# Four warming matmuls instead of nine, filter rows early, and V kept per row: a reordered prologue of a deformable-convolution and spectral-filter kernel

## The reference, cut to what matters

```python
x = x + _L0_conv_ref(_ln_c(x), offset_w, offset_b, mask_w, mask_b, weight, gamma, beta, mean, var)
t = _to_tokens(x)
t = t + _L0_ffn_ref(_ln_t(t), sigma, phi, M_u, M_phi_plus, M_phi_minus, log_weights, gumbel)
x = _from_tokens(t, x)
...
# in _L0_conv_ref: sample 4 corners for each of 9 taps at learned offsets, weigh by ly, lx and a mask
out = deform_conv2d(x, offset, mask, weight, s, p)
scale = bn_gamma / jnp.sqrt(bn_var + BN_EPS)
out = (out - bn_mean) * scale + bn_beta
return out * jax.nn.sigmoid(out)
# in _L0_ffn_ref, for four branches of different length, chosen by a softmax with a hard maximum
s = sigma ** 0.25
out = einsum('btkd,k,kde->bte', U_plus, s, Mpp) + einsum('btkd,k,kde->bte', U_minus, s, Mpm)
out = out + sum_i einsum('btd,de->bte', shift(u, i), Mu[i])          # i = 0, 1, 2
```

## Time and profile before

| what | us |
|---|---|
| median of 3 runs (754.41 to 762.09) | 757.35 |
| profiled execution, its own time | 751.24 |
| span of the profiled execution | 749.4 |
| mean granted TensorE clock | 0.784 |
| busy in the span: PE, PEld, DVE, ACT, POOL | 506.5, 376.8, 314.9, 179.7, 292.7 |
| the chain that ended last: PE, unknown queue, issue, DVE, ACT | 55%, 25%, 10%, 5%, 4% |

### The profile page before, as it was taken

How to read it: one execution, slowest core, us unless ns; L and a number is a source line. 1 busy time by engine, 2 the same in 40 slices (tenths; PEclk the granted TensorE clock), 3 DMA queues, 4 the chain that set the end, 5 groups by cost and what they waited for, 6 DMA issues and landing times.

```text
span 749.4 us, 13126 instructions
## 1 busy us (share of the span) xinstructions
PE 506.5 (68%) x5598; PEld 376.8 (50%) x5598; DVE 314.9 (42%) x800; ACT 179.7 (24%) x421; POOL 292.7 (39%) x295
## 2 busy tenths in 40 slices
PE   5976429246208845785889549891168648999998
PEld 3443105135106613564678329771156327788997
DVE  6467411868602703850438007187009025753000
ACT  1121012113004302321232102240033113334322
POOL 1257750634770372556253732237702745000000
PEclk9966558659557966986999759996569759899999
DMA  8526373811330131222121320113300321000000
GB/s 166 127 79 158 101 204 117 282 56 50 98 105 2 46 107 45 66 71 85 44 64 37 100 64 23 44 44 98 98 21 30 105 64 56 16 2 3 9 2 9
DMA packets 43778, 54.27 MB, mean 72 GB/s; under 512 B 24664, under 2 KB 34142, under 8 KB 43721
## 3 DMA queue, kind: packets, MB, share of 16 engines
q0 software_dynamic: 13824, 37.77, 17.1%
q1 hardware_dynamic: 23841, 13.42, 6.9%
q10 hardware_dynamic: 6056, 2.26, 1.3%
HBM read 50.12 MB, written 3.30 MB: 71 GB/s over the span
## 4 chain that ended last, share of the span: by engine, by line
PE 55%; another core or an unknown queue 25%; issue 10%; DVE 5%; ACT 4%; DMA 1%; SPq 0%; ACTq 0%; DVEq 0%
PE bank L888 30%; PE bank L900 7%; PE bank L760 2%; PE bank L834 2%; PE bank L824 2%; ACT u_conv L661 2%; PE bank L793 2%; PE bank L741 1%; PE bank L795 1%; PE bank L732 1%; PE bank L845 1%; PE bank L919 1%; ACT vT L628 1%; DMA filt<-in_L_ffn_phi_dram 1%
## 5 line engine op out<-in xcount | busy, mean ns | idle before, releaser
L269 POOL DMA_INDIRECT G<-corner_table,idx x288 | 290.0, 1007 | 343.9 <-DVE idx L362 155.2
L888 PE MATMUL bank<-filt,u_hi 128*64 128x256 f16 x2560 | 255.3, 291 | 135.1 <-issue 85.6
L888 PEld LDWEIGHTS bank<-filt,u_hi 128*64 128x64 f16 x2560 | 152.8, 114 | 172.0 <-issue 112.0
L888 PE MATMUL bank<-filt,u_lo 128*64 128x256 f16 x1280 | 198.9, 291 | 15.1 <-issue 15.1
L661 ACT ACTIVATE u_conv<-bank,f_scale 128x256 f32<-128x256 f32 x256 | 118.6, 474 | 303.8 <-PE bank L888 153.6
L900 PE MATMUL bank<-u_conv,mixw 128*64 128x256 f32 (+1 forms) x640 | 94.2, 377 | 9.9 <-issue 9.2
L888 PEld LDWEIGHTS bank<-filt,u_lo 128*64 128x64 f16 x1280 | 84.3, 117 | 24.6 <-issue 22.4
L455 DVE TENSOR_TENSOR G<-G,bank 128x2304 f32<-128x2304 f32 x32 | 81.5, 2548 | 0.3
L467 DVE TENSOR_SCALAR expo<-expo 128x128 f32<-128x128 f32 x16 | 3.6, 227 | 183.1 <-ACT expo L638 172.1
L459 DVE TENSOR_TENSOR V<-G 128x576 f32<-128x576 f32 x32 | 24.3, 758 | 110.0 <-PE bank L825 73.4
L900 PEld LDWEIGHTS bank<-u_conv,mixw 128*64 128x64 f32 x640 | 47.9, 155 | 20.5 <-issue 18.9
(11 more groups left out here) (158 smaller groups left out, 387.3 us busy)
## 6 DMA issues: line engine op xcount, KB each, us to landing
filt<-filter_rows SPq DMA_DIRECT2D x16, 514.0 KB, 9.1
G<-corner_table,idx POOLq DMA_INDIRECT x288
corner_table<-n_uT SPq DMA_DIRECT2D x12, 128.0 KB, 2.9
mixw<-in_x_dram SPq DMA_DIRECT2D x2, 512.0 KB, 6.0
filt<-in_L_ffn_M_phi_plus_dram SPq DMA_DIRECT2D x8, 128.0 KB, 4.9
out_dram<-o_sb ACTq DMA_DIRECT2D x8, 128.0 KB
filt<-n_L_ffn_M_phi_minus_dram ACTq DMA_DIRECT2D x4, 128.0 KB, 4.0
corner_table<-n_uT ACTq DMA_DIRECT2D x4, 128.0 KB, 3.3
```

The costliest lines, as they stand in the source:

```text
L269: pool.indirect_dma_start(G[:, k, tap, :], None, corners[bp], bass.IndirectOffsetOnAxis(ap=idx[:, q % 2, k, tap:tap + 1], axis=0)).then_in ...
L888: last = pe.matmul(conv_ps[b2][C * src:C * src + C, 0:2 * P].rearrange("c (p a) -> c p a", p=2), u[:, NJ * bp + j2, b2, src], h, start=(j2 ...
```

## The change

The change reorders the prologue and removes some of its steps.

- `WARM_UP` is 4 instead of 9.
- The filter rows are made on DVE between the first two `positions`, and the branch weights after the second; the copy of the filter rows to HBM goes ahead of pair 1's tables in SP's queue.
- `weigh(0, 0, 0)` comes ahead of pair 1's layer norm, and `weigh(0, 0, 1)`, positions and weights of unit 1 behind it.
- `V` is kept for each row p. The write of V waits for the turn of the row before the last, and `weigh(0, 1, 0)` and `weigh(0, 1, 1)` stand ahead of the offsets of pair 1 and of both `finish`.
- The roots of the two batch-norm variances and of sigma are one chain over 128 x 80 elements (`roots`), in the place of three. `spectrum_scales` has one chain left, and stands between the two `weigh(0, 1, ...)`.
- On PE the product for the filter scales moves from ahead of row 0 to behind it.
- `u_conv` and `w_diag` share one tile (`late_tiles`), which has no instruction of its own.

```diff
-WARM_UP = 9
+WARM_UP = 4
...
-        V = sb("V", [P, 2, TAPS * C])
+        V = sb("V", [P, 2, 2, TAPS * C])
...
+        roots = sb("roots", [P, 3, C + K])
...
(sync)
+            sp.wait_ge(f_rows_ready, 1)
+            sp.dma_start(ap(hankel, 0, [[4 * HROW, K], [1, 4 * HROW]]), f_rows.rearrange("k p h c -> k (p h c)")
+                         ).then_inc(f_rows_stored, 16)
             for b2 in range(2):
                 for cy in range(2):
                     store_image(sp, 1, b2, cy)
...
-            sp.wait_ge(f_rows_ready, 1)
-            sp.dma_start(ap(hankel, 0, ...
             sp.wait_ge(f_rows_stored, 16)
             load_filters(range(8))
...
(vector)
+            def inverse_roots():
+                dve.wait_ge(s_bn, 16 * 7)
+                link(dve.tensor_scalar(roots[:, 0, 0:C], roots[:, 0, 0:C], BN_EPS, None, ALU.add))
+                rsqrt(roots[:, 1], roots[:, 0], roots[:, 2])
...
                 if b2 == 0:
-                    dve.wait_ge(val_turned, START + 2 * q + p)
-                dve.tensor_tensor(V[:, b2]...
+                    dve.wait_ge(val_turned, START + 2 * q + p - 1)
+                dve.tensor_tensor(V[:, p, b2]...
...
             branch_logits()
+            dve.memset(vT[C:C + 1, :, 4, :], 1.0).then_inc(ones_ready, 1)
             offsets(0, 0)
             positions(0, slice(0, BLK, 2))
-            branch_weights()
+            filter_rows()
             offsets(0, 1)
             positions(0, slice(1, BLK, 2))
+            branch_weights()
             masks(0)
             weights(0)
+            weigh(0, 0, 0)
+            normalise_pixels(1, (0, 1))
+            weigh(0, 0, 1)
             positions(1)
             weights(1)
-            normalise_pixels(1, (0, 1))
-            weigh(0, 0, 0)
+            inverse_roots()
             main_weights()
-            weigh(0, 0, 1)
-            filter_rows()
+            weigh(0, 1, 0)
+            spectrum_scales()
+            weigh(0, 1, 1)
             offsets(1, 0)
             offsets(1, 1)
-            dve.wait_ge(n_ready, 3)
-            dve.memset(vT[C:C + 1, :, 4, :], 1.0).then_inc(ones_ready, 1)
-            weigh(0, 1, 0)
             finish(0, 0)
-            weigh(0, 1, 1)
-            spectrum_scales()
             dve.wait_ge(f_scale_ready, 1)
...
(tensor)
-            pe.wait_ge(diag_ready, 1)
-            pe.wait_ge(off_copied, 2 * BP)
-            pe.matmul(scale_ps[:, 0:K], ones[:], f_diag[:], start=True, stop=True).then_inc(f_scale_ready, 1)
...
-            for r in range(2):
-                turn_values(r)
-                convolve_values(r)
-                turn_convolved(r)
+            turn_values(0)
+            convolve_values(0)
+            turn_convolved(0)
+            pe.wait_ge(diag_ready, 1)
+            pe.wait_ge(off_copied, 2 * BP)
+            pe.matmul(scale_ps[:, 0:K], ones[:], f_diag[:], start=True, stop=True).then_inc(f_scale_ready, 1)
+            turn_values(1)
+            convolve_values(1)
+            turn_convolved(1)
```

More of the change, by code:

```diff
@@ L108, in metaformer_kernel @@
         f_diag = sb("f_diag", [K, K])
-        sig = sb("sig", [P, 4, K])
+        sig = sb("sig", [P, 3, K])
+        roots = sb("roots", [P, 3, C + K])
         f_scale = sb("f_scale", [P, K])
         br = sb("br", [P, 10, BRANCHES])
-        w_diag = sb("w_diag", [P, BRANCHES, 3, P])
         mu_raw = sb("mu_raw", [C, BRANCHES, 3 * C])
         mu = sb("mu", [P, 4, 3, C])
-        u_conv = sb("u_conv", [P, 2, 2, 2, P])
+        late_tiles = sb("late_tiles", [P, 1536])
+        u_conv = late_tiles[:, 0:1024].rearrange("s (k b p a) -> s k b p a", k=2, b=2, p=2)
+        w_diag = late_tiles[:].rearrange("s (r v d) -> s r v d", r=BRANCHES, v=3)
         o_sb = sb("o_sb", [P, 2, 2 * P])
@@ L185, in metaformer_kernel @@
         pool_marks, pe_marks, dve_marks, act_marks = (sem(f"{n}_marks") for n in ("pool", "pe", "dve", "act"))
-        N_SMALL = 3
+        N_SMALL = 2
         N_MATS = 5 * BRANCHES
@@ L295, in _ @@
             dve.memset(ones[:], 1.0).then_inc(ones_ready, 1)
+            dve.memset(roots[:, 0, 0:C], 1.0).then_inc(roots_set, 1)
             dve.memset(f_rows, 0.0)
@@ L425, in main_weights @@
                 dve.wait_ge(s_w, 16)
-                link(dve.tensor_scalar(bn_col[:, 1:2], bn_col[:, 1:2], BN_EPS, None, ALU.add))
-                rsqrt(st2[0:C, 0, 0:1], bn_col[:, 1:2], st2[0:C, 1, 0:1])
-                link(dve.tensor_tensor(bn_col[:, 0:1], bn_col[:, 0:1], st2[0:C, 0, 0:1], ALU.mult))
+                link(dve.tensor_tensor(bn_col[:, 0:1], bn_col[:, 0:1], roots[0:C, 1, 0:1], ALU.mult))
                 dve.tensor_scalar(w_scaled[:].rearrange("o (t c) -> o t c", t=TAPS),
@@ L457, in weigh @@
                 if b2 == 0:
-                    dve.wait_ge(val_turned, START + 2 * q + p)
-                dve.tensor_tensor(V[:, b2].rearrange("s (t c) -> s t c", c=C), G[:, k, :, 0:C], G[:, k, :, C:2 * C], ALU.add
+                    dve.wait_ge(val_turned, START + 2 * q + p - 1)
+                dve.tensor_tensor(V[:, p, b2].rearrange("s (t c) -> s t c", c=C), G[:, k, :, 0:C], G[:, k, :, C:2 * C], ALU.add
                                   ).then_inc(v_ready[b2], 1)
@@ L549, in _ @@
         def _(act):
-            for i, v in enumerate((sigma, log_weights, gumbel)):
-                dst = sig[:, 0, :] if i == 0 else br[:, i - 1, :]
-                act.dma_start(dst, ap(v, 0, [[0, P], [1, K if i == 0 else BRANCHES]])).then_inc(s_small, 16)
+            for i, v in enumerate((log_weights, gumbel)):
+                act.dma_start(br[:, i, :], ap(v, 0, [[0, P], [1, BRANCHES]])).then_inc(s_small, 16)
             act.dma_start(w_raw, ap(weight, 0, [[C * TAPS, C], [1, C * TAPS]])).then_inc(s_w, 16)
-            for i, v in enumerate((gamma, var)):
-                act.dma_start(bn_col[:, i:i + 1], ap(v, 0, [[1, C], [1, 1]])).then_inc(s_bn, 16)
-            for i, v in enumerate((gamma, beta, mean, var)):
+            act.dma_start(roots[:, 0, C:C + K], ap(sigma, 0, [[0, P], [1, K]])).then_inc(s_bn, 16)
+            act.dma_start(bn_col[:, 0:1], ap(gamma, 0, [[1, C], [1, 1]])).then_inc(s_bn, 16)
+            for i, v in enumerate((gamma, beta, mean)):
                 act.dma_start(bn_row[C:C + 1, i, :], ap(v, 0, [[C, 1], [1, C]])).then_inc(s_bn, 16)
+            act.wait_ge(roots_set, 1)
+            act.dma_start(roots[0:C, 0, 0:1], ap(var, 0, [[1, C], [1, 1]])).then_inc(s_bn, 16)
+            act.dma_start(roots[C:C + 1, 0, 0:C], ap(var, 0, [[C, 1], [1, C]])).then_inc(s_bn, 16)
             for s in (u_copied, *conv_copied):
@@ L823, in turn_values @@
                     for m in range(4):
-                        pe.transpose(val_ps[b2][:, P * m:P * m + P], V[:, b2, P * m:P * m + P], ident)
-                    last = pe.transpose(tail_ps[0:C, P * b2:P * b2 + P], V[:, b2, 4 * P:4 * P + C], ident)
+                        pe.transpose(val_ps[b2][:, P * m:P * m + P], V[:, r % 2, b2, P * m:P * m + P], ident)
+                    last = pe.transpose(tail_ps[0:C, P * b2:P * b2 + P], V[:, r % 2, b2, 4 * P:4 * P + C], ident)
                 last.then_inc(val_turned, 1)
```

19 lines of the change are left out of this document (6 added, 13 removed).

## The result

The changed kernel took 767.11 us (median of 4 runs, 763.87 to 771.99); the kernel before, on the same chip beside it, 755.88 (748.04 to 762.09). The ratio is 1.018, with a 95% interval of 1.011 to 1.026: slower by 1.8%. The profiled execution of the change has a span of 766.7 us, against 749.4. The kernel before itself had medians from 756 to 770 us in the different calls, so times of different calls are compared by their ratios; where this text compares stages, it compares single traces.

What follows compares the result with a forecast made beforehand. Gather streams nearly stopping PE's hand-overs to ACT were taken as the bound. Pair 1 19 us later, rows 0 and 1 13.5 less, passes +1: +6.5, added as 6 to the median 757.35 for 763 us; range 742 to 772.

Steps and rivals of the forecast that it cites:

- Warming: Start of the prologue: ten warming pieces fewer on PE bring everything to the second indices and gather streams 3.3 us earlier.
- V per row takes POOL's pause: Prologue: DVE writes V without waiting for PE, so POOL's pause of 28.8 us between two gather streams goes.
- The stream of 63: Prologue: 45 and 18 gathers join into one stream of 81 us, from 44.8 to 126 us.
- The hold's own rule: Under gather streams: after 14 us PE's hand-overs nearly stand still, 8.8 us each; cleared about 5 us behind the last gather.
- harmless 14 us: A gather stream's first 14 us were taken not to slow PE's hand-overs to ACT, which need 2 us each there.
- Pair 1 starts at 132.5: Prologue: PE starts pair 1 behind the merged stream, 19 us later than 113.58; bounds 117 and 140.
- Rows 0 and 1: Prologue, pair 1's offsets to first convolution: row 1 is turned sooner as its V stands, 13.5 us less; bounds 10 and 15.5.
- Passes: Pass 2, unit 4: nine gathers join the 18 before them; between -2 and +4 us, taken as +1.
- Rival B: Prologue: DVE's small steps are slowed too, V comes late and breaks the long stream; no change, 757 us; chance 0.22.
- A: Prologue: the stalls don't follow the gathers, so pair 1 isn't held and the kernel is faster, 745.6 us; chance 0.27.
- C: Passes: two or three more streams merge, 11 us each; with one more such unit 774 us; chance 0.09.

Runs made afterwards that it cites:

- e4: The changed kernel with nine warming matmuls again in place of four; 782.78 us, ratio 1.026 to the kernel before.
- e11: The changed kernel run and traced once more without any edit; 778.03 us, ratio 1.011 to the kernel before.
- e1: The changed kernel, with POOL waiting after each slot's nine gathers until the last has landed; 684.97 us, ratio 0.896 to the kernel before.
- e12: The changed kernel, bursts of 5 and 4 gathers, rests of four memsets for units 0 and 1, waits for the landing from unit 2; 603.49 us, ratio 0.799.
- e6: The changed kernel, with POOL waiting for the landing after the fifth and ninth gather of each slot; 627.37 us, ratio 0.817 to the kernel before.
- e10: The changed kernel, bursts of 5 and 4 gathers, with four linked memsets as the rest and no wait for a landing; 634.02 us, ratio 0.820.
- e2: The changed kernel, with POOL starting unit 1's gathers only when PE has turned pair 1's offsets; 765.34 us, ratio 0.999 to the kernel before.
- e9: The changed kernel, with POOL waiting for the landing after every sixth gather, counted through the slots; 644.31 us, ratio 0.836.

## Why the prediction was right, and where it was not

The forecast, 763, is 4 us under the measured 767, and the direction and the cause (gathers that run on where they had waited for V, and hold what stands under them) were right. The size was half of what came: +6 us was forecast, +11.2 measured between the medians, +17.3 between the two traces. The range of +1 to +13 is not what its own bounds add up to either; they give −14 to +20. Its steps fared unevenly.

- *Warming, −3.3.* L745 at 16.57 and the first gather at 29.12, as forecast (16.7, 29.3). e4 prices it at 3.0 us at the first gather and 1.6 to 2.7 at the first convolution.
- *V per row takes POOL's pause.* Right in kind: the wait of 28.8 us for V is gone. The stream of 63 was not there in the first trace; in e11 it was, but for one rest of 2.8 us behind its 54th gather.
- *The hold's own rule.* The harmless 14 us don't hold in general: in a burst of pass 2 in e1, PE issues 38 matmuls in the first 7 us from 274 and 7 in the next 3, from 8.3 us into the burst on. Of the earlier trace rows I wrote that only POOL works and PE runs at a ninth of the speed; DVE is busy for 9.8 us there, and 26 matmuls in 33 us against 227 in 27 is an eleventh.
- *Pair 1 starts at 132.5.* This step failed. PE turned pair 1 at 93 in one trace and from 102 in the other, outside my bounds of 117 to 140. I had priced a hand-over at 8.8 us throughout; e11 shows 4 us at a stream's age of 28 us and 10.7 at 55, so more got through early. What I had not seen is that the work behind, the copies or the convolution itself, would then be held by what gathers were left. The end of the stage came out right all the same, offsets at 146.7 and 149.0 where 147 was forecast: in the first trace the convolution itself was caught, and the offsets stood 8.6 us behind the last gather (138.1); in e11 the copies ahead of it were, and 19.2 us were needed behind the last gather (129.8). A right sum by a wrong path, and so luck.
- *Rows 0 and 1, −13.5.* Right in kind. In the first trace it was −9.4, because row 0's exponential came 10.5 us behind the offsets, not 7.0; in e11 it was −13.5 (22.4 us from the offsets to the first convolution in place of 35.9). Row 1 follows row 0 after 9.1 and 8.5 us, where 8.5 was forecast, and after 9.1 in e1.
- *Passes, +1.* It was +8.9 in pass 2 and +8.1 in all, above my bound of +4, and it stood in the one place that I named, unit 4's streams. I had said that the shorter stream's earlier end would pay for the pause; the whole nine-gather block of 11 us was lost but for 2.
- *Rival B's argument.* I held DVE's steps over 128 partitions to be exempt, for L456 started on time. They aren't. Under the first stream:

```profile
56.00 1.05 DVE L351 RECIPROCAL mask<-mask 128x144 f32<-128x144 f32 x1 [6.82 <-remote]
```

  L377 and L457 behind it waited 5.78 and 4.38 us in the same way, and so unit 1's indices came at 91.8, not at 74.2 as in e11, and POOL rested for 17.3 us. In e11 it was B's own picture, small steps 1.4 us apart (above), and V was whole at 118.6 us, between the forecast's 92 and B's 128. The row I took for an exception in the kernel before was the first of several:

```profile
75.65 0.15 DVE L290 TENSOR_TENSOR st<-st,bn_col 64x1 f32<-64x1 f32 x1 [1.25 <-issue]
78.45 0.15 DVE L290 TENSOR_TENSOR st<-st,bn_col 64x1 f32<-64x1 f32 x1 [1.25 <-DVE st L289]
```

  What L456 had was not its 128 partitions but the step ahead of it, L455, which takes 2.5 us. I read these rows so: under an old stream an engine starts something only each 0.7 or 1.4 us, which long instructions hardly feel. That is argued from three stretches (PE in the first trace, DVE in e11 and in the kernel before), not tested, and the waits of 4 to 7 us above are more than it explains. B's mechanism was at work in both traces, without its gain.
- *Rivals A and C.* A fell with 33 pieces of L764 in 35 us, where nothing in the code holds them. C's further streams did not merge; its price of about one nine-gather block is what the one merged stream cost.

The larger miss is outside the sum. I read the earlier trace rows as a price list for streams and moved it about, and did not ask what the hold costs in all. e12 puts a lower bound to it: rests alone took the changed kernel's span from 766.7 to 603.9 us, by 162.8, and 145.5 of the 749.4 us of the kernel before are gone with the change and the rests together.

What stays open is why a stream slows PE. It isn't the amount moved (77 and 78 GB/s in e1 and e6), and no landing has to be waited for to get most of the gain (e10). The Trainium skill, SBUF — State Buffer (SBUF: two separate sides), says that a DMA can't be slowed by a compute instruction, nor the other way round, because their ports are separate. Read as a statement on the whole, these traces don't agree: one piece of L764 started per 1.40 us under a stream, where all 72 took 7.9 us in e2 without one. Whether the ports have a part in it, no run tests. The Trainium skill's NOTIFIC — the notification-queue block (7.1 Overflow: three behaviours, one of which stalls the engine) describes records of instructions whose inner pipeline never drops one and can so throttle an engine; no run here shows whether that is at work.

## What to carry to other kernels

When one engine issues a long row of small indirect transfers, look at what the others do under it and in the first microseconds behind it. If small instructions that wait for nobody start 0.7 or 1.4 us apart, break the row with rests before you reorder anything: with 63 rests of 1.5 to 2 us the changed kernel was 20% faster than the kernel before, where the reordering alone had cost 1.8%. And a change that takes a wait away is priced by what the freed engine then does, for the wait may have been the rest that the others lived on.

## What the runs showed of the hardware

- The shorter a burst of gathers, the less it holds PE, down to 5 and 4 (6.3 us and less). Pass 3 took 94 us with bursts of 9 (e1), 81 with 6 (e9) and 74 with 5 and 4 (e6), the last with more gathers in it. Even there pass 2 takes 67 us, where pass 6 without gathers takes 50 in e1, with 731 matmuls in both; how much of that is POOL's own pace is open.
- A rest of 1.5 us does in the prologue (first convolution at 115.4 and 112.3 in e10 and e12); passes 2 and 3 do better with waits for the landing, some 2.0 us (67 and 71 us against 82 and 83). Length and landing aren't told apart.
- Under an old stream short instructions start 1.4 us apart, on PE (L764, 103 to 138 us of the change) and on DVE (the roots of sigma in e11). An instruction behind a long one was on time there; L457 in the first trace was 4.4 us late all the same.
- The hold of hand-overs from PE to ACT deepens with a stream's age, from 4 to 10.7 us between ages of 28 and 55 us in e11, with one of 22 at the end, and is paid off 4 to 6 us behind the last gather (142.12 against 138.1, 135.66 against 129.8).
- While PE crawls, the granted clock is 0.51 (the lower of the two levels, 1.2 GHz; 103 to 138 us of the change); from 250 to 310 us it is 0.70 in e1 and 0.94 in e6.
